# A bias that moves from GpSimd to TensorE: the output bias of the first attention in a two-layer decoder

## The reference

```python
x = x + _L0_attn_ref(_layernorm(x), ...)          # recurrent block with a decay
x = x + _L0_xattn_ref(_layernorm(x), ctx, ctx, ...)
...
def _L0_xattn_ref(q, k, v, Wq1, bq1, ..., Wo, bo):
    qh, kh, vh = (tanh(t @ W1 + b1) @ W2 + b2 for t in (q, k, v), head by head)
    attn = softmax(qh @ kh.T / sqrt(16))
    ctx = (attn @ vh) with the heads side by side
    return ctx @ Wo + bo
```

## Time and profile before

| | us |
|---|---|
| median of 3 runs (5405.54 to 5415.52) | 5413.46 |
| the profiled execution, its own time | 5405.82 |
| span in the profile | 5403.9 |
| TensorE, matmul, busy | 4731.9 (88%) |
| VectorE busy | 4303.5 (80%) |
| GpSimd busy | 3938.4 (73%) |
| ScalarE busy | 2323.7 (43%) |

### The profile page before, as it was taken

One profiled execution on the slowest core, in us unless ns is written; L12 is line 12 of the kernel. 1 busy time (PEld: TensorE's weight loads), 2 busy tenths in 40 slices (PEclk: granted clock), 3 DMA queues, 4 the chain that ended last, 5 costly groups with the idle time before them and its releaser, 6 DMA issues.

```text
span 5403.9 us, 105986 instructions
## 1 busy us (share of the span) xinstructions
PE 4731.9 (88%) x28362; PEld 3086.5 (57%) x28362; DVE 4303.5 (80%) x11377; ACT 2323.7 (43%) x4480; POOL 3938.4 (73%) x10789
## 2 busy tenths in 40 slices
PE   1089999999999999999999999998999999899999
PEld 0065656656565565656556565664656556565655
DVE  8878788787878877787877778777787887878788
ACT  0044444454444444443444544445444444444444
POOL 7478686777868678686767868676785867778686
PEclk7599999999999999999999999999999999999999
DMA  3000000000000000000000000000000000000000
GB/s 89 8 13 9 21 1 25 5 9 21 1 29 1 25 5 9 21 1 29 1 13 17 9 21 1 25 5 9 21 9 21 1 25 5 9 21 1 21 1 17
DMA packets 61894, 78.20 MB, mean 14 GB/s; under 512 B 11168, under 2 KB 53808, under 8 KB 61232
## 3 DMA queue, kind: packets, MB, share of 16 engines
q1 hardware_dynamic: 52784, 62.42, 3.6%
q10 hardware_dynamic: 8448, 8.39, 0.4%
HBM read 45.04 MB, written 8.46 MB: 10 GB/s over the span
## 4 chain that ended last, share of the span: by engine, by line
PE 33%; POOL 29%; DVE 21%; issue 11%; ACT 4%; POOLq 2%; DMA 0%; DVEq 0%; ACTq 0%; SPq 0%
POOL acc_c L635 11%; POOL arena L635 6%; PE bank L1331 3%; PE bank L1238 3%; POOL acc_a L635 3%; POOL acc_b L635 3%; POOL acc_s L635 3%; POOL sl_t L635 2%; PE bank L1191 2%; DVE arena L2088 2%; PE bank L1067 2%; POOLq L634 2%; PE bank L1074 2%; PE bank L1157 2%; PE bank L1143 2%
## 5 line engine op out<-in xcount | busy, mean ns | idle before, releaser
L1854 DVE TENSOR_REDUCE smax<-bank 128x4 f32<-128x512 f32 x768 | 525.2, 684 | 92.3 <-PE bank L1149 51.0
L817 ACT ACTIVATE arena<-bank 128x512 f32<-128x512 f32 x768 | 454.9, 592 | 249.4 <-PE bank L1157 243.7
L1858 DVE TENSOR_TENSOR arena<-bank,smax 128x512 f32<-128x512 f32 x768 | 531.2, 692 | 26.4
L1157 PE MATMUL bank<-ident,arena 128*128 128x128 f32 x3072 | 485.8, 281 | 43.0 <-ACT arena L804 25.7
L1238 PE MATMUL bank<-w,arena 128*128 128x512 f32 x1024 | 490.4, 610 | 14.0 <-DVE arena L1806 14.0
L1143 PE MATMUL bank<-arena 64*128 64x512 f32 x1536 | 440.2, 650 | 64.4 <-ACT arena L841 28.0
L1157 PEld LDWEIGHTS bank<-ident,arena 128*128 128x128 f32 x3072 | 346.9, 141 | 242.9 <-ACT arena L806 82.2
L1271 PE MATMUL bank<-w,arena 128*128 128x256 f32 x2048 | 454.1, 380 | 13.9 <-ACT arena L876 13.9
L804 ACT ACTIVATE arena<-arena,rstd 128x512 f32<-128x512 f32 x512 | 368.1, 719 | 197.9 <-DVE arena L1858 193.4
L1271 PEld LDWEIGHTS bank<-w,arena 128*128 128x128 f32 x2048 | 387.8, 190 | 90.3 <-issue 23.0
L635 POOL TENSOR_TENSOR acc_a<-acc_s,arena 128x32 f32<-128x32 f32 x1008 | 262.1, 260 | 175.4 <-DVE gate L1973 51.8
(11 more groups left out here) (437 smaller groups left out, 11962.0 us busy)
## 6 DMA issues: line engine op xcount, KB each, us to landing
arena<-in_x_dram SPq DMA_DIRECT2D x35, 512.0 KB, 3.6
xn_next<-arena SPq DMA_DIRECT2D x17, 512.0 KB, 2.9
arena<-cum_dram SPq DMA_DIRECT2D x17, 512.0 KB, 3.8
arena<-in_ctx_dram SPq DMA_DIRECT2D x16, 512.0 KB, 3.7
out_dram<-arena ACTq DMA_DIRECT2D x16, 512.0 KB, 3.1
xn<-xn_next SPq DMA_DIRECT2D x15, 512.0 KB, 3.0
w<-in_L_ffn_w_dram SPq DMA_DIRECT2D x8, 512.0 KB
w<-in_L_ffn_w_dram SPq DMA_DIRECT2D x1, 1024.0 KB
```

Source lines behind the costliest of these rows:

```text
L817: act.activation(PT[:, v % 2], bank[3 + v % 2][:, :].rearrange("p (h q) -> p h q", h=QH), ACT.Copy).then_inc(S["pt"], 1)
L1157: ins = tr(bank[3 + v % 2][:, j * P:(j + 1) * P], Ssb[:, v % 4, j, :], ident[:, :])
L1854: dve.tensor_reduce(smax[:, u, :], sc, AX, ALU.max).then_inc(S["s_max"], 1)
L1858: dve.tensor_tensor(Ssb[:, u % 4], sc, smax[:, u, :].unsqueeze(2).broadcast_to([P, QH, P]), ALU.subtract).then_inc(S["s_sub"], 1)
```

## The change

GpSimd's instruction L656 goes. In its place, at u = QUADS + 2 = 18 of the first attention, TensorE multiplies a column of ones (`ones_row`, 1 x 128, written once by GpSimd before the loop) by the bias row, repeated twice (1 x 512), into bank 0 and into bank 1, with start and without stop. The four projections of this attention then add to what stands in the banks. VectorE's first wait for `bias_res` goes, and the second counts one instead of two. In the arithmetic `bo` is now added ahead of the projection's sum.

```diff
-    res=10, bias_res=2, xin_used=1,
+    res=10, bias_res=1, xin_used=1,
...
+        ones_row = sb("ones_row", [1, P])
...
+            link(pool.memset(ones_row[:, :], 1.0))
...
                 pool.wait_ge(S["xn"], at(it, "xn", 4))
-                pool.tensor_tensor(xres[:, :, :], xres[:, :, :], bo_row[:, :].unsqueeze(1).broadcast_to([P, G, D]), ALU.add).then_inc(S["bias_res"], 1)
                 pool.wait_ge(ref_step, nth(it, REF_STEPS, REF_BEFORE + ROOT_STEPS))
...
+                        if a_no == 0 and u == QUADS + 2:
+                            for m in range(2):
+                                mm(bank[m][:, :], ones_row[0:1, :], bo_row[0:1, :].unsqueeze(1).broadcast_to([1, 2, D]), start=True, stop=False)
...
-                        ins = mm(bank[g // 2][:, (g % 2) * D:(g % 2 + 1) * D], attT[:, c, g * P:(g + 1) * P], w_out[:, c, :], start=(c == 0), stop=(c == C - 1))
+                        ins = mm(bank[g // 2][:, (g % 2) * D:(g % 2 + 1) * D], attT[:, c, g * P:(g + 1) * P], w_out[:, c, :], start=(c == 0 and a_no > 0), stop=(c == C - 1 and (a_no > 0 or g % 2 == 1)))
...
                 attention(0)
-                wait("bias_res", 1)
...
-                    wait("bias_res", 2)
+                    wait("bias_res", 1)
...
-SET_POOL = 62
+SET_POOL = 63
```

## The result

| | before | after |
|---|---|---|
| median, six runs of each | 5414.49 us | 5452.91 us |
| range | 5405.54 to 5416.10 | 5446.94 to 5454.98 |
| the profiled execution | 5405.82 | 5449.15 |
| span in the profile | 5403.9 | 5447.3 |
| TensorE, matmul, busy | 4731.9 | 4763.9 |

What follows compares the result with a forecast made beforehand. No single engine was taken as the bound; the chain runs through TensorE, VectorE, ScalarE and GpSimd. The products' 1.73 us less 0.54 us at the router gave 16 x 1.19 = 19.0 us on 5413.5 us: 5432.5 us, range 5415 to 5450 us.

Steps and rivals of the forecast that it cites:

- L656 worth nothing: GpSimd's `bo_row` addition, 2.36 us a pass (37.7 us in all), lies ahead of waits, so removing it gains nothing.
- L1446's 0.83 us: VectorE's small sum is held up 0.83 us by L656; without it exact_root and GpSimd's links come 0.83 us earlier.
- The products' price S: Two fp32 products on TensorE's chain in the first attention cost 1.73 us a pass; bounds half of it and 1.9 us.
- The row of 8 rows: L1345, 8 rows and 256 columns, 374 ns against 379 ns with 128 rows: few rows save next to nothing.
- The router as a wall: At the router L663's end sets the time: L1910 caught, weights 1.19 us later for any shift from 1.01 to 2.13 us.
- the step to L1960: At the router, a shift over 2.13 us gets L1960 caught by the bias addition; the rise would be 36 us.
- The step that failed: Behind the last transpose TensorE has no gap, so everything up to the router shifts 1.73 us; sixteen times, 27.7 us.
- The term of the sum: Router's weights, and GpSimd's sum behind them, come 1.19 us later in each of 16 passes: 19.0 us.
- a second step: Behind the router's weights nothing is added; the wait for `au` covers most of TensorE's further 0.54 us.
- The clock as a rival: Third attention's tail: changed pass lengths shift the clock's pattern, 5407 to 5458 us; chance 0.11 much given back, 0.06 all.
- a sign of being wrong: New records under 1.01 us, router's hold-up vanishing, or the part behind `au` changing by over 1 us on average.
- The rival on the other side: Products cheap or hidden, under 1.01 us: router's weights +0.32 us a pass, 5.1 us in all, 5418.6 us; chance 0.13.

Runs made afterwards that it cites:

- experiment 2: The kernel before without L656 and its wait, the bias `bo` left out altogether: 5423.31 us, ratio 1.0009.
- experiment 7: The changed kernel with products of 128 rows at u = 16 and the `onb_row` addition two link groups earlier on GpSimd: 5408.93 us, ratio 0.9991.
- experiment 8: The changed kernel with three bf16 bias parts on 96 rows, two bf16 products at u = 16, `onb_row` addition two link groups earlier: 5397.96 us, ratio 0.9976.
- Experiment 10: The changed kernel with three bf16 bias parts on 96 rows, two bf16 products at u = 16, `onb_row` addition at its old place: 5403.78 us, ratio 0.9981.
- experiment 6: The kernel before with the `onb_row` addition two link groups earlier on GpSimd, nothing else: 5404.05 us, ratio 0.9983.
- experiments 9 and 12: The changed kernel with 128 weight rows, 127 of them zero (9): 5443.18 us, ratio 1.0051; with 32 rows of 1/32 (12): 5454.32 us, ratio 1.0080.

## Why the prediction was wrong

**L656 worth nothing: right.** Its 2.36 us became waiting, and experiment 2 measures 1.0009.

**L1446's 0.83 us: right.** The instruction takes 0.15 us, and GpSimd's L664 starts 0.80 us earlier (55.14 us behind L830 on average, 55.94 before).

**The products' price S: nearly right.** "I take 1.73 us" was read from L1205 with 128 rows. With 128 rows they do take 1.72 us, with 1, 8 or 32 rows 1.91 us, which was the upper bound, "with a gap"; the gap is the 0.17 us in front of the first load of weights. The row of 8 rows showed that few rows save nothing; it did not show that they cost more.

**The router as a wall: right, and shown in several places.** The old L1910 is caught in the passes with a quiet clock, and the weights come 1.1 us late against 1.19 forecast. Which instruction is caught, and how late the router ends, follow VectorE's lateness in order:

| kernel | caught in the pass shown | weights behind L830 |
|---|---|---|
| before | L1927, the mask's product | 60.9 |
| no bias, pass 1 | a comparison of ranks | 61.0 |
| full rows, u = 16 | the product with `grc` | 61.1 |
| full rows, u = 18 | L1913, subtraction of the maximum | 62.0 |
| 32 rows, pass 1 | L1963, `hrs` | 62.9 |
| changed kernel, pass 1 | L1766, `parts` | 63.9 |

The prediction named the step to L1960 too, from a lateness over 2.13 us. With 32 rows L1963 starts 55.14 us behind L831 (396.38 - 341.24), where L1960 started 52.97 us behind L830: 2.17 us late, and caught. In pass 2 of the changed kernel it is 2.05 us late, and passes. So the bound held; the lateness at that point is 0.1 to 0.3 us more than the products' own 1.91 us.

**The step that failed** is this one: "so there is no gap to hide in, and everything behind shifts by S = 1.73 us: the first expert's products, VectorE's moments, the router. Sixteen times, 27.7 us." It treats the products as time only. They also changed TensorE's granted clock right behind them, in half of the passes, and there the shift is 1.91 + 1.6 us, not 1.73. The term of the sum that this made wrong is 16 x 1.19 = 19.0 us: ahead of the router's weights the profiled executions differ by 32.3 us, about 8 x 1.1 in the passes without the fall and 8 x 3.0 in those with it. That is 13.3 of the missing 24.3 us (43.3 - 19.0).

The rest is a second step, that the sum has no term behind the weights: 8.8 us came behind `au` and 3.8 between the weights and `au` (the first and the last stage take 1.5 us back). The 3.8 us, 0.24 us a pass, weren't followed further. The 8.8 us go with the granted clock of the third attention. In the kernel before, five of the fifteen stages behind `au` take 111.3 to 111.4 us, with the lower clock for 6.8 us; in the changed kernel none is under 112.6, and nine take 113.1 to 113.2, with the lower clock for 10.2 us. Two such stages as windows, the first of the kernel before and the second of the changed one:

```profile
547.61:658.98 111.37, 102.69 (x594) 78.29 (x594) 86.55 (x272) 39.64 (x70) 64.37 (x117) 0.97 0.08 25
```
```profile
871.51:984.66 113.15, 104.29 (x593) 78.87 (x594) 86.00 (x273) 39.47 (x69) 62.37 (x117) 0.95 0.08 25
```

What puts the clock on one course or the other there is not shown. The profiled execution of before has the stage at 112.9 us on average, where ten of the thirteen others have 113.4 to 114.2, and its time is 8.7 us under the median, so part of the 8.8 us is the pattern that this one execution happened to meet. By the medians the rise was 38 us and 19 us were missing.

**The clock as a rival: half right.** The prediction looked for it at the tail of the third attention, where it was low before, and let it follow the passes' length. There it did cost something, but 0.585 us a pass, less than the 1 us that the prediction named as a sign of being wrong. It didn't ask whether the new instructions themselves would let the clock fall ahead of the router.

The Trainium skill's page "TensorE: Matmul & The Clock Gate", section "Part 1: The HAM clock gate", ties the clock to how busy TensorE has been, and its cases of a fall from 2.4 to 1.2 GHz come from an engine that waits. Here the records fill the stretch ahead of the fall, and its rows are what differs between a fall and none. The rule of its section "Why this matters for your kernels", that a product of few rows takes a full one's time, stands a little low, by the 1.91 us against 1.72.

The Trainium skill's page "SBUF — State Buffer", section "SBUF: two separate sides", has the other half right: an instruction with two SBUF inputs and one of GpSimd exclude each other for the whole instruction. In every pass of every kernel here but experiment 7, where the addition runs beside instructions that read PSUM, and three passes of experiment 8, one short instruction of VectorE was held up by the `onb_row` addition, and it ended 0.02 to 0.04 us behind it.

**The rival on the other side** wanted products of under 1.01 us. Experiment 10 made them so, with two records of 0.38 us at u = 16, and then the time is indeed no longer than before (0.9981).

## What to carry to other kernels

A bias by TensorE was not paid in columns alone here. Feed all 128 rows (the bias on every partition, weights of 1/128) or bf16 parts, and look at the granted clock right behind the new product, pass by pass. Where a GpSimd instruction runs beside a chain of small VectorE instructions that read SBUF alone, list these with their starts against the start of the GpSimd instruction, and price the change by which one will be caught; moving the GpSimd instruction can be worth more than removing another (0.9983 for the move of experiment 6, 1.0009 for the removal of experiment 2). Compare stages pass by pass as well as whole times: one profiled execution can lie 9 us off its kernel's median. And before taking work off an engine, see whether that engine waits right behind it: here 2.36 us a pass were worth nothing.

## What was not expected of the hardware

- Behind two fp32 products of few rows TensorE's granted clock fell, with no wait on its timeline for the 5 us ahead of the fall (3 us at the earlier place): 8 of 16 passes with 1 row, 11 with 8, none with 32 or 128, none with 128 rows whose weights are zero in 127; at the earlier place 16 of 16 with 1 row and none with 128.
- Two fp32 products of 512 columns take 1.91 us with 1, 8 or 32 rows and 1.72 us with 128; with few rows the first load of weights starts 0.17 us late.
- The passes can lock into a pattern: one row at u = 16 gives thirteen passes of 324.2 to 324.3 us.
- `au` earlier by 1.1 us (experiment 7) went with a stage behind it that is 1.9 us longer than in the one profiled execution of before. How long that stage is goes with how long the lower clock lasts in it (experiments 9 and 12: 10.2 us against 13.7, 113.0 to 113.2 us against 115.3 to 115.6). What decides between them stays open.
